# Cross attention block, one core: the first two chunks of scores of a group start behind the turns and the first feed-forward product

## The chip, the cores and the metric

The kernel runs on one core of one Trainium2 chip. Times are device microseconds of the whole execution; the median of three runs of the kernel before is 1809.25 us (1807.23 to 1810.44). The engines are TensorE (PE, with its weight loads as PEld), VectorE (DVE), ScalarE (ACT), GpSimd (POOL) and SyncE (SP), whose queue issues the DMAs.

## The reference, cut to what matters

```python
# x, memory: (128, 128, 256); mask (128, 128, 128); 16 heads of 16; FF = 1024
def _self_attn(x, mask, ...):
    q = (x @ Wq.T + bq).reshape(b, s, H, HD)      # k, v likewise
    score = jnp.einsum('bshd,bthd->bhst', q, k) / math.sqrt(HD)
    score = score + (1.0 - mask[:, None, :, :]) * -1000000000.0
    p = jax.nn.softmax(score, axis=-1)
    o = jnp.einsum('bhst,bthd->bshd', p, v).reshape(b, s, d)
    return o @ Wo.T + bo
tgt1 = _layer_norm(tgt, g1, be1)
tgt = tgt + _self_attn(tgt1, mask, ...)
tgt = tgt + (memory @ Wg.T + bg)
tgt1 = _layer_norm(tgt, g2, be2)
ff = jax.nn.relu(tgt1 @ W1.T + b1) @ W2.T + b2
return tgt + ff
```

## The kernel before, in words

The 128 sequences are taken in 64 groups of two (256 rows). The work of a group is spread over several iterations of one loop, as a software pipeline: iteration i makes the first layer norm of group i + 2, turns and projects q, k and v of group i + 1 ("front"), makes the scores and exponentials of group i ("attn_"), the values, output projection and second layer norm of group i - 1 ("out_"), and the feed-forward part of group i - 2 ("ffn"). An iteration has 13 ticks (TICKS), and each engine has its own list by tick, written out by hand; the tables at the top of the file say at which tick a step stands. An engine works its list strictly in that order, and semaphores join the lists. No scheduler moves anything.

Products keep float32 accuracy with three matmuls each: operands are split into a high and a low part (xT_hi and xT_lo, and so on), and `product` makes low x high, high x low and high x high (L807 to L809). For the scores the same is done by stacking: q and k of a group are copied by nine DMAs of SyncE into q_stack (three) and k_stack (six), so that one matmul multiplies all three pairs. These copies are issued when VectorE has made the low parts q_lo and k_lo (L648, L656).

The scores of a group are 8 chunks of four heads. `scores_of(i, n)` (L859) makes chunk n with two matmuls into bank n % 2 of score_ps. Chunk 0 waits for the copies (q_stacked, k_stacked). Each chunk waits until VectorE has read the chunk two before it, which used the same bank (scores_masked). VectorE masks a chunk and takes the row minimum with four instructions (L608, after a small memset, L605); behind chunk 0's masking its list has xT_lo, the low part of the next group's turned input (L571), which the q product needs. ScalarE makes the exponentials of a chunk (L374), and between them the high parts (L367, L436, L445), the relu of the feed-forward tiles (L419) and the copies of turned tiles (L386, L394). TensorE turns a chunk of exponentials (`turn_chunk`, L873), the inverse sums (`turn_inverses`, L883), and xhat for the next group (`turn`, L824).

`up(i, t)` makes two of the eight tiles of the first feed-forward product, 12 matmuls into ffn_ps; at tick 0 it waits for z_split and for y_summed, with which VectorE has read ffn_ps of the group before (L593). At tick 1 stand chunk 2's scores, then the values of the group before (L899) and the q product.

Of the kernel before, what the change touches and what calls it, by code (L numbers as in the profile page):

```python
# [53 lines left out]
def later(g):  # L54

    return not (isinstance(g, int) and g == 0)

def is_at(i, n):

    return isinstance(i, int) and i == n
# [7 lines left out]
def xattn_block(nc, x, memory, mask, wqT, wkT, wvT, woT, wgT, w1T, w2T,  # L69
# [24 lines left out]
    with ExitStack() as ctx:  # L94
# [685 lines left out]
        def _(pe):  # L780
# [22 lines left out]
            def product(dst, pairs, start=True, stop=True, **more):  # L803

                n = len(pairs)
                for j, (lhs, rhs) in enumerate(pairs):
                    pe.matmul(dst, lhs[1], rhs[0], start=start and j == 0, stop=False, **more)  # L807
                    pe.matmul(dst, lhs[0], rhs[1], start=False, stop=False, **more)  # L808
                    last = pe.matmul(dst, lhs[0], rhs[0], start=False, stop=stop and j == n - 1, **more)  # L809
                return last  # L810

            def cut(pair, *at):
                return pair[0][at], pair[1][at]
# [3 lines left out]
            def seq(b):  # L817
                return slice(b * S, (b + 1) * S)
# [8 lines left out]
            def up(i, t):  # L827

                g, n = i - 2, UP_TICKS.index(t)
                if is_at(i, 2) and n == 0:  # L830
                    pe.wait_ge(split_lo, SPLIT_AT["1"])
                    pe.wait_ge(split_more, MORE_AT["2"])
                if n == 0:
                    pe.wait_ge(z_split, g + 1)
                    if later(g):
                        pe.wait_ge(y_summed, g)
                else:
                    pe.wait_ge(hid_relu, HJ * g + n)
                for j in range(2):
                    f = 2 * n + j  # L840
                    last = product(ffn_ps[:, j * ROWS:(j + 1) * ROWS],
                                   [(cut(w1, ALL, k, slice(f * P, (f + 1) * P)), cut(zT, ALL, k))
                                    for k in range(KT)])
                last.then_inc(hid_ready, 1)

            def scores_of(i, n):

                b, c = divmod(n, CPB)
                if b == 0:
                    if c == 0:  # L850
                        if i < 2:
                            pe.wait_ge(zeros_set, 2 * i + 2)
                        pe.wait_ge(q_stacked, 16 * TERMS * (i + 1))
                        pe.wait_ge(k_stacked, 16 * 2 * TERMS * (i + 1))
                if n >= 2 or later(i):
                    pe.wait_ge(scores_masked, CHUNKS * i + n - 1)

                for k in range(KT):
                    last = pe.matmul(score_ps[n % 2][:, k * 2 * S:(k + 1) * 2 * S],  # L859
                                     q_stack[i % 2][:, c, k, seq(b)],  # L860
                                     k_stack[i % 2][:, c, :, GB * k + b, :],
                                     start=True, stop=True)
                last.then_inc(scores_ready, 1)
# [41 lines left out]
            def iteration(i, norm, front, attn_, out_, ffn):  # L905
                fronts, outs = stages_before(i)
                for t in range(TICKS):
                    if attn_ and t == 0:
                        scores_of(i, 0)
                        scores_of(i, 1)  # L910
                    if attn_ and t in SCORE_TICKS:
                        scores_of(i, SCORE_TICKS[t])
                    if attn_ and t in TURN_TICKS:
# [8 lines left out]
                        turn(by_tile[1], xhat).then_inc(x_turned, 1)  # L922
                    if ffn and t in UP_TICKS:
                        up(i, t)
                    if attn_ and t == 1:
                        scores_of(i, 2)
                    if out_ and t == 1:
# [61 lines left out]
            for name in "qk":  # L989
                shift_product(name)  # L990
            pe.wait_ge(ident_loaded, 16)
            run(pe, iteration)

# [34 lines left out]
```

## Time and profile before

| what | value |
|---|---|
| median of three runs | 1809.25 us |
| the profiled execution | 1808.42 us |
| its span | 1806.8 us |
| TensorE busy | 1752.8 us, 97% |
| ScalarE busy | 1455.3 us, 81% |
| VectorE busy | 1356.8 us, 75% |
| GpSimd busy | 876.4 us, 49% |
| mean DMA rate | 102 GB/s |

A time of the trace is counted from the span's start. A row that stands for several instructions (x4) gives the start of the first and the time until the last one's end. A matmul's record is longer than the distance to the next matmul, since they are pipelined. In brackets stands how long the engine was idle before the row, and what ended that; short idle times carry no bracket.

### The profile page before, as it was taken

To read this page: it belongs to the slowest core of one execution; us is meant where nothing else is said; L and a number is where in the kernel's file an instruction comes from.
4 is the path that set the end of the run, shared out by engine and by line. 5 is a ranking of instruction groups with operands and counts; after the bars stand their busy time and mean duration, and the time that the engine had idled before them with its cause. 6 is when DMAs were issued, how large, how long until landed. Compare 5 with 4: busy or idle time off the path is not lost.

```text
span 1806.8 us, 53745 instructions
## 1 busy us (share of the span) xinstructions
PE 1752.8 (97%) x17972; PEld 1717.7 (95%) x17972; DVE 1356.8 (75%) x6807; ACT 1455.3 (81%) x5577; POOL 876.4 (49%) x910
## 2 busy tenths in 40 slices
PE   5699999999999999999999999999999999999997
PEld 5699999999999999999999999999999999999997
DVE  6677777777777777777777777777777777777772
ACT  4788888787787887888787887887888888887882
POOL 4254454454454455455454454444544444454454
PEclk7899999999999999999999999999999999999999
DMA  7665765755765755755755755755755756756740
GB/s 165 94 94 99 119 93 99 118 92 98 121 91 95 124 89 98 123 89 99 124 88 99 123 88 100 123 87 101 124 85 101 121 87 103 117 90 104 112 72 19
DMA packets 148931, 183.66 MB, mean 102 GB/s; under 512 B 14768, under 2 KB 99120, under 8 KB 148656
## 3 DMA queue, kind: packets, MB, share of 16 engines
q1 hardware_dynamic: 148656, 180.23, 60.6%
q8 instruction: 144, 2.36, 0.6%
q14 instruction: 131, 1.07, 0.2%
HBM read 62.73 MB, written 16.78 MB: 44 GB/s over the span
## 4 chain that ended last, share of the span: by engine, by line
PE 94%; ACT 1%; issue 1%; DMA 0%; DVE 0%; SPq 0%; ACTq 0%
PE ffn_ps L807 13%; PE ffn_ps L808 13%; PE ffn_ps L809 13%; PE turn_ps L873 12%; PE work_ps L807 9%; PE work_ps L809 8%; PE work_ps L808 8%; PE score_ps L859 7%; PE value_ps L899 6%; PE work_ps L824 3%; PE turn_ps L883 2%; ACT scores L374 1%; DMA k_stack<-k_hi 0%; ACT hid L419 0%; SPq L325 0%
## 5 line engine op out<-in xcount | busy, mean ns | idle before, releaser
L374 ACT ACTIVATE scores<-scores,row_min 128x128 f32<-128x128 f32 x2048 | 795.4, 402 | 0.8 <-DVE row_min L608 0.8
L733 POOL TENSOR_TENSOR hT_lo<-hid,hT_hi 128x512 fp32r<-128x512 f32 x256 | 355.5, 1389 | 552.5 <-DVE hT_hi L635 552.5
L386 ACT ACTIVATE probs<-turn_ps 128x512 f32<-128x512 f32 x512 | 305.2, 597 | 254.7 <-PE turn_ps L873 254.7
L608 DVE CUSTOM_DVE_ANT_0 scores<-score_ps,mask_bias 128x128 f32<-128x128 f32 x2048 | 471.5, 286 | 1.9 <-issue 1.9
L374 ACT ACTIVATION_READ_ACCUMULATOR scores<-scores,row_min 128x1 f32 x2048 | 412.7, 202 | 0.0
L873 PE MATMUL turn_ps<-ident,scores 128*128 128x128 f32 x2048 | 308.3, 273 | 5.9 <-ACT probs L386 5.9
L807 PE MATMUL ffn_ps<-zT_hi,w_lo 128*128 128x256 f32 x1024 | 302.3, 295 | 5.0 <-ACT hid L419 4.1
L807 PE MATMUL ffn_ps<-w_hi,hT_lo 128*128 128x256 f32 x1024 | 300.7, 294 | 2.4 <-ACT hid L419 2.4
L808 PE MATMUL ffn_ps<-zT_lo,w_hi 128*128 128x256 f32 x1024 | 285.5, 279 | 0.0
L809 PE MATMUL ffn_ps<-zT_hi,w_hi 128*128 128x256 f32 x1024 | 284.9, 278 | 0.0
L809 PE MATMUL ffn_ps<-w_hi,hT_hi 128*128 128x256 f32 x1024 | 284.6, 278 | 0.0
L808 PE MATMUL ffn_ps<-w_lo,hT_hi 128*128 128x256 f32 x1024 | 284.4, 278 | 0.0
L873 PEld LDWEIGHTS turn_ps<-ident,scores 128*128 128x128 f32 x2048 | 234.8, 140 | 7.2 <-ACT scores L374 6.6
L635 DVE CAST hT_hi<-hid 128x512 fp32r<-128x512 f32 x256 | 110.1, 430 | 160.3 <-ACT hid L419 160.2
L419 ACT ACTIVATE hid<-ffn_ps,vec 128x256 f32<-128x256 f32 x512 | 212.6, 468 | 18.0 <-PE ffn_ps L809 17.9
L859 PE MATMUL score_ps<-k_stack,q_stack 128*128 128x256 f32 x1024 | 199.8, 288 | 24.7 <-issue 13.9
L807 PEld LDWEIGHTS ffn_ps<-zT_hi,w_lo 128*128 128x128 f32 x1024 | 193.9, 189 | 6.6 <-ACT hid L419 5.1
L807 PEld LDWEIGHTS ffn_ps<-w_hi,hT_lo 128*128 128x128 f32 x1024 | 192.7, 188 | 3.0 <-ACT hid L419 3.0
L808 PEld LDWEIGHTS ffn_ps<-w_lo,hT_hi 128*128 128x128 f32 x1024 | 193.8, 189 | 0.0
L808 PEld LDWEIGHTS ffn_ps<-zT_lo,w_hi 128*128 128x128 f32 x1024 | 193.8, 189 | 0.0
L809 PEld LDWEIGHTS ffn_ps<-zT_hi,w_hi 128*128 128x128 f32 x1024 | 192.8, 188 | 0.0
L809 PEld LDWEIGHTS ffn_ps<-w_hi,hT_hi 128*128 128x128 f32 x1024 | 192.2, 188 | 0.0
(113 smaller groups left out, 4242.2 us busy)
## 6 DMA issues: line engine op xcount, KB each, us to landing
q_stack<-q_hi SPq DMA_DIRECT2D x128, 256.0 KB, 6.8
k_stack<-k_hi SPq DMA_DIRECT2D x256, 128.0 KB, 7.3
x_in<-x_dram SPq DMA_DIRECT2D x64, 256.0 KB, 3.7
mem_in<-memory_dram SPq DMA_DIRECT2D x64, 256.0 KB, 7.9
x_res<-x_dram SPq DMA_DIRECT2D x64, 256.0 KB, 7.9
q_stack<-q_lo SPq DMA_DIRECT2D x64, 256.0 KB, 4.2
k_stack<-k_lo SPq DMA_DIRECT2D x128, 128.0 KB, 7.3
out_dram<-y SPq DMA_DIRECT2D x64, 256.0 KB, 2.2
```

Of the source, the lines that this page charges most:

```text
L374: last = act.activation(exps, exps, ACT.Exp, bias=row_min[:, k, h:h + 1], scale=-1.0, accum_out=row_sum[:, k, h:h + 1])
L386: act.activation(probs[:, k, :], turn_ps[k % 2][:, :], ACT.Copy).then_inc(probs_copied, 1)
L419: last = act.activation(hid[:, n % 2, j, :], ffn_ps[:, j * ROWS:(j + 1) * ROWS], ACT.Relu, bias=b1c[:, 2 * n + j:2 * n + j + 1])
L608: last = dve.tensor_tensor_reduce(out=scores[:, slot(i, t), h, :], in0=score_ps[t % 2][:, h * S:(h + 1) * S], in1=mask_bias[:, b, :], scal ...
L635: dve.tensor_copy(hT[0][:, 2 * n:2 * n + 2, :], hid[:, n % 2]).then_inc(hid_hi, 1)
L733: pool.tensor_tensor(halves[1], src, halves[0], ALU.subtract).then_inc(done, 1)
L807: pe.matmul(dst, lhs[1], rhs[0], start=start and j == 0, stop=False, **more)
L808: pe.matmul(dst, lhs[0], rhs[1], start=False, stop=False, **more)
L809: last = pe.matmul(dst, lhs[0], rhs[0], start=False, stop=stop and j == n - 1, **more)
L859: last = pe.matmul(score_ps[n % 2][:, k * 2 * S:(k + 1) * 2 * S], q_stack[i % 2][:, c, k, seq(b)], k_stack[i % 2][:, c, :, GB * k + b, :], ...
L873: last = pe.transpose(turn_ps[k % 2][:, h * S:(h + 1) * S], scores[:, slot(g, k), h, :], ident[:])
L899: last = pe.matmul(value_tiles[32 * c:32 * (c + 1), k, seq(b)], v_pad[g % 2][:, b, head_of(c, h), :], probs[:, CPB * b + c, h * S:(h + 1) ...
```

## The change

On TensorE alone, the scores of chunks 0 and 1 are no longer first in tick 0. They stand at the end of tick 0: behind the turn of the last group's chunk 7, the turn of its inverse sums, the turn of xhat and the first two feed-forward tiles. Chunk 2 stays at tick 1, and so stands right behind them. The lists of the other engines, and what each step waits for, are the same.

```diff
             def iteration(i, norm, front, attn_, out_, ffn):
                 fronts, outs = stages_before(i)
                 for t in range(TICKS):
-                    if attn_ and t == 0:
-                        scores_of(i, 0)
-                        scores_of(i, 1)
                     if attn_ and t in SCORE_TICKS:
                         scores_of(i, SCORE_TICKS[t])
                     if attn_ and t in TURN_TICKS:
...
                         turn(by_tile[1], xhat).then_inc(x_turned, 1)
                     if ffn and t in UP_TICKS:
                         up(i, t)
+                    if attn_ and t == 0:
+                        scores_of(i, 0)
+                        scores_of(i, 1)
                     if attn_ and t == 1:
                         scores_of(i, 2)
                     if out_ and t == 1:
```

The first place is TensorE's list where an iteration begins, behind the last matmul of the group's second feed-forward product. Before:

```order
L809 MATMUL ffn_ps<-w2_hi,hT_hi 128x256
L859 MATMUL score_ps0<-k_stack1,q_stack1 128x256 [waits scores_masked,k_stacked,q_stacked]
L859 MATMUL score_ps0<-k_stack1,q_stack1 128x256
L859 MATMUL score_ps1<-k_stack1,q_stack1 128x256 [waits scores_masked]
L859 MATMUL score_ps1<-k_stack1,q_stack1 128x256
L873 MATMUL turn_ps1<-ident,scores 128x128 [waits probs_copied,exps_ready]
L873 MATMUL turn_ps1<-ident,scores 128x128 x3
```

And of the kernel after the change:

```order
L809 MATMUL ffn_ps<-w2_hi,hT_hi 128x256
L873 MATMUL turn_ps1<-ident,scores 128x128 [waits probs_copied,exps_ready]
L873 MATMUL turn_ps1<-ident,scores 128x128 x3
L883 MATMUL turn_ps0<-ident,inv_rows 128x128 [waits probs_copied,inv_spread]
L883 MATMUL turn_ps0<-ident,inv_rows 128x128 x3
L824 MATMUL work_ps1<-ident,xhat 128x128 [waits z_split,ln1_ready]
L824 MATMUL work_ps1<-ident,xhat 128x128 x3
L807 MATMUL ffn_ps<-zT_hi,w1_lo 128x256 [waits y_summed,z_split]
```

The four score matmuls, with their wait for the copies, are gone from here; the turns follow the second product at once.

The second place is the end of the 12 matmuls of the first feed-forward product and what follows. Before:

```order
L809 MATMUL ffn_ps<-zT_hi,w1_hi 128x256
L859 MATMUL score_ps0<-k_stack1,q_stack1 128x256 [waits scores_masked]
L859 MATMUL score_ps0<-k_stack1,q_stack1 128x256
L899 MATMUL value_ps<-probs,v_pad0 32x128 [waits attn_ready,values_set,probs_copied]
L899 MATMUL value_ps<-probs,v_pad0 32x128 x31
L807 MATMUL work_ps1<-xT_hi,wq_lo 128x256 [waits x_split]
```

And after the change:

```order
L809 MATMUL ffn_ps<-zT_hi,w1_hi 128x256
L859 MATMUL score_ps0<-k_stack1,q_stack1 128x256 [waits scores_masked,k_stacked,q_stacked]
L859 MATMUL score_ps0<-k_stack1,q_stack1 128x256
L859 MATMUL score_ps1<-k_stack1,q_stack1 128x256 [waits scores_masked]
L859 MATMUL score_ps1<-k_stack1,q_stack1 128x256
L859 MATMUL score_ps0<-k_stack1,q_stack1 128x256 [waits scores_masked]
L859 MATMUL score_ps0<-k_stack1,q_stack1 128x256
L899 MATMUL value_ps<-probs,v_pad0 32x128 [waits attn_ready,values_set,probs_copied]
```

Chunks 0, 1 and 2 now stand in a row. The last of them goes to score_ps0, the bank of the first.

## Rows read from the trace of the kernel before

**Rows 1.** The page: its head, and the chain that ended last by engine.

```profile
span 1806.8 us, 53745 instructions
...
PE 94%; ACT 1%; issue 1%; DMA 0%; DVE 0%; SPq 0%; ACTq 0%
```

**Rows 2.** The table of waits: total us, times, longest us.

```profile
PEld score_ps L859 <- issue: 31.9, 49, 5.2
```

**Rows 3.** Timeline of PEld, a group's first scores: start, us, operation, [idle before].

```profile
112.23 0.53 PEld L859 LDWEIGHTS score_ps<-k_stack,q_stack 128*128 128x128 f32 x4 [0.40 <-issue]
...
818.64 0.53 PEld L859 LDWEIGHTS score_ps<-k_stack,q_stack 128*128 128x128 f32 x4 [0.17 <-issue]
...
845.44 0.55 PEld L859 LDWEIGHTS score_ps<-k_stack,q_stack 128*128 128x128 f32 x4
...
1742.35 0.53 PEld L859 LDWEIGHTS score_ps<-k_stack,q_stack 128*128 128x128 f32 x4 [0.42 <-issue]
```

**Rows 4.** Timeline of PE at the start of the group at 845.55 us.

```profile
845.55 0.64 PE L859 MATMUL score_ps<-k_stack,q_stack 128*128 128x256 f32 x4
...
846.03 0.60 PE L873 MATMUL turn_ps<-ident,scores 128*128 128x128 f32 x4
...
847.26 0.36 PE L807 MATMUL ffn_ps<-zT_hi,w_lo 128*128 128x256 f32 x1
...
848.63 0.28 PE L809 MATMUL ffn_ps<-zT_hi,w_hi 128*128 128x256 f32 x1
...
848.75 0.40 PE L859 MATMUL score_ps<-k_stack,q_stack 128*128 128x256 f32 x2
```

**Rows 5.** Timeline of a group whose scores and masks both waited, 655.3 to 657.6 us.

```profile
655.62 0.53 PEld L859 LDWEIGHTS score_ps<-k_stack,q_stack 128*128 128x128 f32 x4 [0.60 <-issue]
655.65 0.71 PE L859 MATMUL score_ps<-k_stack,q_stack 128*128 128x256 f32 x4 [0.42 <-issue]
...
656.21 0.60 PE L873 MATMUL turn_ps<-ident,scores 128*128 128x128 f32 x4
...
656.30 0.06 DVE L605 MEMSET carrier<- 128x1 f32 x1 [0.33 <-PE score_ps L859]
...
657.18 0.08 DVE L608 DVE_READ_ACCUMULATOR2_ANT row_min<- 128x1 f32 x1
```

**Rows 6.** Timeline, 45.5 to 47.5 us: scores that waited for VectorE.

```profile
46.01 0.08 DVE L608 DVE_READ_ACCUMULATOR2_ANT row_min<- 128x1 f32 x1
...
46.15 0.30 PEld L859 LDWEIGHTS score_ps<-k_stack,q_stack 128*128 128x128 f32 x2 [0.70 <-DVE row_min L608]
```

**Rows 7.** Timeline of VectorE and ScalarE, 845.3 to 849.6 us.

```profile
845.75 0.69 DVE L593 TENSOR_TENSOR y<-ffn_ps,resid_b 128x512 f32<-128x512 f32 x1
...
848.03 0.39 ACT L374 ACTIVATE scores<-scores,row_min 128x128 f32<-128x128 f32 x1
...
848.17 0.69 DVE L571 TENSOR_TENSOR xT_lo<-work_ps,xT_hi 128x512 fp32r<-128x512 f32 x1 [0.87 <-ACT xT_hi L367]
```

**Rows 8.** Timelines of ACT and PEld between 825 and 830 us.

```profile
825.83 0.84 ACT L436 ACTIVATE q_hi<-work_ps,qk_bias 128x256 fp32r<-128x256 f32 x2 [0.24 <-PE work_ps L809]
...
828.10 0.83 ACT L419 ACTIVATE hid<-ffn_ps,vec 128x256 f32<-128x256 f32 x2
...
829.61 0.19 PEld L807 LDWEIGHTS ffn_ps<-zT_hi,w_lo 128*128 128x128 f32 x1
```

**Rows 9.** Timelines of VectorE and PE in the first groups.

```profile
55.94 2.34 DVE L543 TENSOR_SCALAR xhat<-x_in,mv,rstd 128x256 f32<-128x256 f32 x2
...
82.38 1.20 PE L859 MATMUL score_ps<-k_stack,q_stack 128*128 128x256 f32 x4 [4.38 <-issue]
...
88.18 0.39 PE L859 MATMUL score_ps<-k_stack,q_stack 128*128 128x256 f32 x2
```

**Rows 10.** The tail: PE's timeline; stretch, busy PE PEld DVE ACT POOL, clock, DMA.

```profile
1789.96 0.38 PE L807 MATMUL ffn_ps<-zT_hi,w_lo 128*128 128x256 f32 x1 [0.93 <-ACT hid L419]
...
1784.00:1800.00 16.00, 11.41 (x91) 10.44 (x90) 3.10 (x6) 3.96 (x9) 6.83 (x6) 1.00 0.05 18
```

## The prediction

> **What bounds the kernel now.** I read the page first. TensorE carries 94% of the chain that ended last, and no other engine more than 1% [rows 1]. So a microsecond in which TensorE waits is a microsecond of time, and one that another engine gains or loses counts only where TensorE waits for it. The second view is the table of waits: beside the start-up, TensorE's repeated wait is ahead of the scores (49 times, 31.9 us, put down to "issue") [rows 2]. The third view is the row of the four score matmuls that open a group. They stand once a group, and their weight loads start at 112.23 us for group 3 and at 1742.35 us for group 63: 60 periods of (1742.35 - 112.23) / 60 = 27.17 us [rows 3]. Of these 60 starts, 44 carry a mark of an idle stretch of 0.17 to 0.60 us. The start at 845.44 us carries none, and its period is 845.44 - 818.64 = 26.80 us [rows 3]. The code says what it is: the first chunk waits for the six copies into k_stack, and these land just about when TensorE gets there.
>
> **What the change removes.** The two chunks that wait for those copies are started later: behind three sets of four turns and behind the two tiles of the first feed-forward product. In the group without a wait the scores take 846.03 - 845.55 = 0.48 us, the turns 847.26 - 846.03 = 1.23 us and the product 848.75 - 847.26 = 1.49 us [rows 4]. The copies thus get 1.23 + 1.49 = 2.72 us more, where they were at most 0.6 us late. I show below that their issue slides by at most about 1.5 us relative to a group's start, while a whole period grows too; so this wait goes. Its worth: the free period is 26.80 us from load to load, but a load that has waited stands 0.08 us nearer to its matmul, so from matmul to matmul it is up to 26.88 us. The gain is 0.29 to 0.37 us a group, middle 0.33; times 61 groups (3 to 63) that is 20 us, bounds 18 to 22.
>
> **What the change adds.** score_ps has two banks. Chunk 2 writes the bank of chunk 0 and waits for scores_masked, that is for VectorE to have read chunk 0. Before, 2.72 us of other matmuls stood between chunk 1 and chunk 2, and the wait was met long before. Now chunk 2 stands right behind chunk 1 (second pair of order fences), and nothing covers it. I lay this out on the times of [rows 4]. The turns start where the scores did, at 845.55. The product starts 0.48 earlier than it did, at 846.78, and its last matmul at 848.63 - 0.48 = 848.15. Chunk 0's two matmuls start at 848.27 and 848.39, and the second ends 0.28 later, at 848.67. Chunk 1 is through TensorE's order at 848.75, the very time at which chunk 2 started before, since it is the same work in another order.
>
> How long VectorE then needs is shown by a group in which VectorE stood waiting for the scores [rows 5]. The four matmuls there start at 655.65 and the last at 655.65 + 0.71 - 0.28 = 656.08, so chunk 0's second started near 655.84 and ended near 656.12; VectorE's first instruction starts at 656.30, a hop of 0.18 us. Its last accumulator read ends at 657.18 + 0.08 = 657.26, which makes 0.96 us for a chunk. From VectorE's end to the weight load that waited for it the trace has one clean place: 46.01 + 0.08 = 46.09 to 46.15, 0.06 us [rows 6]. Chunk 2's load is released at 848.67 + 0.18 + 0.96 + 0.06 = 849.87, that is 1.12 us behind 848.75. A load that is released by a wait isn't done ahead of time: in [rows 5] it takes 656.21 - 655.62 = 0.59 us from the load to the next group of matmuls, where 0.48 is usual. That is 0.11 us more. The stall is 1.12 + 0.11 = 1.23 us; with a hop of 0.14 in place of 0.18 it is 1.19, and without the restart it is 1.08. I take 1.2 us, bounds 1.05 to 1.3. Times 61 groups: 73 us, bounds 64 to 79.
>
> **What is queued behind it.** VectorE must be free when chunk 0 lands: its sum for the output y runs from 845.75 to 846.44 [rows 7], and nothing else of its list stands before chunk 0's masking, so it is. The same sum frees ffn_ps for the product, which would now start at 846.78; that leaves about 0.3 us, the closest cover on this side. If it fell short, the turns and the product would slide by what lacks, so it is no gain for anyone. Behind the masking stands xT_lo, 0.69 us long, which before ran at 848.17 [rows 7] and now ends near 849.8 + 0.7 = 850.5. The q product needs it, but the 64 matmuls of the values stand ahead of that product and take about 1.9 us from 850.2, so this is hidden.
>
> ScalarE starts chunk 0's exponentials at 848.03 before [rows 7] and near 849.80 now, 1.77 us later; it had idle time ahead of them, and of q_hi another 0.24 us [rows 8]. By q_hi it is some 1.5 us late against 1.2 us of TensorE. The next thing that TensorE wants of it is the second tiles' relu: it runs 828.10 to 828.93, and TensorE's load that needs it starts at 829.61 [rows 8]. Of the 0.68 us between them 0.3 to 0.35 us goes, so it still holds. Through q_lo and k_lo, which follow ScalarE, the copies are issued those 1.5 us later, against 1.2 + 2.72 = 3.9 us later that they are wanted. ScalarE's lateness ends in its idle time near the end of a group, where it waits for turns that TensorE makes late in its order. I cost these at nothing, with 0 to 0.2 us a group (12 us) kept for the upper end.
>
> **The first groups.** Group 0: VectorE is busy with weights, and its first masks start no earlier; nothing. Group 1: xhat for its turns is ready only at 55.94 + 2.34 = 58.28 [rows 9], behind the landing of the copies, so what is saved in one place is lost in the other; nothing. Group 2 waited 4.38 us for its copies; turns and product now run in that time. Its chunk 2 started at 88.18, and would start about 1.8 us behind 82.38 [rows 9], some 4 us earlier. But the exponentials come only about 2.5 us earlier, and some of the values then fall into the stretch at half clock. I take 2.5 us of gain, bounds 0 to 4.
>
> **Sum.** +73 - 20 - 2.5 = +50.5 us. The profiled execution took 1808.42 us with a span of 1806.8 us: 1808.4 + 50.5 = 1859 us. The median of the runs before, 1809.25, lies 0.8 above that execution, which changes nothing here.
>
> **A rule that speaks of such waits.** After the waits of 0.93 us in the last two iterations, the granted clock stayed at 1.00, the 2.4 GHz level, over 1784 to 1800 us though they came every 2.6 us or so [rows 10]; after the 4.38 us wait the same work went at the 1.2 GHz level: from 82.38 to 88.18 = 5.80 us, for what takes 848.75 - 845.55 = 3.20 us otherwise [rows 4, 9]. The Trainium skill, "TensorE: Matmul & The Clock Gate", section "A second HAM failure mode: psum-queue depth-cycling", tells of a kernel in which short idle times between groups of matmuls while the PSUM banks are cycled let the clock swing. By that rule each of the new waits could set the clock back; by the rows of the tail it would not. No trace here has a wait of 1.2 us once a group in the steady part.
>
> **Rivals.**
> 1. The clock falls at each new wait. If each costs what the half clock cost behind 82.38, 5.80 - 3.20 = 2.6 us: 61 x 2.6 = 159 us more, 2018 us. Against it stands the tail [rows 10]. 2%.
> 2. ScalarE becomes a second thing to wait for. Its lateness against TensorE eats more than the 0.68 us of [rows 8], and the feed-forward tiles wait 0.3 to 0.5 us a group: 61 x 0.4 = 24 us more, 1883 us. For it: ScalarE runs without a break from q_hi to the end of the group. Against it: the 0.3 us left. 7%.
> 3. The wait for the copies stays, since q_lo and k_lo slide with ScalarE: then the 20 us aren't gained, 1879 us. It would take a slide of over 3 us. 3%.
> 4. The other side: faster. Chunk 2 isn't held up, because its mark is set before TensorE gets there; then only the gains are left, 1808.4 - 20 - 2.5 = 1786 us. It decides at the second matmul of chunk 0: VectorE's reading would have to end within 0.36 us of its start, where [rows 5, 6] give 0.28 + 0.18 + 0.96 + 0.06 = 1.48. Something between (a stall that later waits give back) would need idle time of TensorE to be paid from, and in the steady part there is hardly any other than the one that I have already counted. 4%, with 1% of it all for a draw.
>
> **How the numbers follow.** My forecast has 83%, the rivals 7, 3, 2 and 4% and a draw 1%. 0.2% (3.6 us) is about what a measurement of this kernel can tell from no change. Slower by more than that: 83 + 7 + 3 + 2 = 95%; within it 1%; faster 4%. The range: all terms low, 64 - 22 - 4 = +38, 1846 us; all high, 79 - 18 + 12 = +73, 1881 us. All at one end at once is unlikely; I let it begin a little lower, at 1844, for a smaller restart and hop, and end at 1878.
>
> **What would show it.** Right: no idle mark ahead of the group's first scores; chunk 2's weight load waiting for row_min at 1.0 to 1.3 us once in every group; VectorE's masks of chunk 0 right behind the first two scores, with idle time before them; periods near 26.84 + 1.2 = 28.0 us; the granted clock at 1.00; the product's and the down product's waits for ScalarE still rare. Wrong: a period under 27.3 us (the stall isn't there or is repaid), one over 28.4 us (rivals 1 or 2), or a wait that still names k_stack.

## The result, and the profile after

| | before | after |
|---|---|---|
| median | 1809.32 us | 1860.62 us (1858.68 to 1862.06, 4 runs) |
| ratio | | 1.0284, 95% interval 1.0266 to 1.0302 |
| profiled execution, its span | 1808.42, 1806.8 us | 1859.95, 1858.3 us |
| period of a group, groups 3 to 63 | 27.17 us | 28.04 us |

The change made the kernel 51.3 us slower, where 50.5 were forecast. Of the experiments below, one execution of e1 (7810.56 us) and one of e4 (1983.98 us, at a granted clock of 0.88, the profiled one, so no row of e4 is shown) were far slower than the others, and the ratios leave them out. In the page after, the chain of work that ended last answers to [rows 1]; VectorE has come into it:

```profile
span 1858.3 us, 53745 instructions
...
PE 92%; DVE 4%; ACT 2%; issue 1%; DVEq 0%; ACTq 0%
```

The table of waits after (total us, times, longest us) answers to [rows 2]. The 49 waits of the first scores are gone, and in their place TensorE's load waits for VectorE at chunk 2 once in every group, with one more in group 0; VectorE waits for the scores and ScalarE for VectorE about as often:

```profile
DVE carrier L605 <- PE score_ps L859: 150.6, 66, 2.8
...
ACT scores L374 <- DVE row_min L608: 137.1, 64, 2.8
PEld score_ps L859 <- DVE row_min L608: 76.1, 65, 2.1
PE score_ps L859 <- DVE row_min L608: 63.1, 65, 1.8
```

The timeline of one group after, from chunk 0's scores to the values, answers to [rows 4, 5]. The row of x4 is chunks 0 and 1 and has no mark of idle time; the next row of PE is chunk 2:

```profile
868.84 0.53 PEld L859 LDWEIGHTS score_ps<-k_stack,q_stack 128*128 128x128 f32 x4
868.95 0.62 PE L859 MATMUL score_ps<-k_stack,q_stack 128*128 128x256 f32 x4
869.50 0.06 DVE L605 MEMSET carrier<- 128x1 f32 x1 [2.35 <-PE score_ps L859]
...
870.39 0.08 DVE L608 DVE_READ_ACCUMULATOR2_ANT row_min<- 128x1 f32 x1
...
870.51 0.40 ACT L374 ACTIVATE scores<-scores,row_min 128x128 f32<-128x128 f32 x1 [2.15 <-DVE row_min L608]
870.53 0.30 PEld L859 LDWEIGHTS score_ps<-k_stack,q_stack 128*128 128x128 f32 x2 [1.17 <-DVE row_min L608]
870.53 0.50 PE L859 MATMUL score_ps<-k_stack,q_stack 128*128 128x256 f32 x2 [0.97 <-DVE row_min L608]
...
870.96 0.43 PE L899 MATMUL value_ps<-probs,v_pad 128*32 128x128 f32 x8
```

VectorE's chain is 870.39 + 0.08 - 869.50 = 0.97 us, and 0.06 us later TensorE's load is released. The mark in the timeline is only 0.97 us, but the stall costs more than its mark. Chunk 1 is through TensorE's order at 868.95 + 0.48 = 869.43, while the record of its last matmul runs to 868.95 + 0.62 = 869.57, so TensorE has nothing to issue for 870.53 - 869.43 = 1.10 us. And the load isn't done ahead: from chunk 2 to the values it takes 870.96 - 870.53 = 0.43 us, where it takes 0.32 us in e2 below, which doesn't wait there.

The granted clock, last but two in the row of the steady stretch, stayed at the 2.4 GHz level with these waits in every group:

```profile
120.00:1780.00 1660.00, 1602.82 (x16572) 1571.68 (x16571) 1232.84 (x6280) 1330.21 (x5154) 793.08 (x829) 1.00 0.61 100
```

### The profile page after: what moved, and what is told of

Its sections match the earlier page's. It is cut to its first block, busy times and chain, and to the rows that moved or that the text cites. A ratio compares the mean times of both kernels' runs of the same rounds, so it can differ in the third digit from the quotient of the medians.

```text
span 1858.3 us, 53745 instructions
## 1 busy us (share of the span) xinstructions
PE 1759.2 (95%) x17972; PEld 1718.1 (92%) x17972; DVE 1348.6 (73%) x6807; ACT 1447.0 (78%) x5577; POOL 876.7 (47%) x910
## 4 chain that ended last, share of the span: by engine, by line
PE 92%; DVE 4%; ACT 2%; issue 1%; DVEq 0%; ACTq 0%
PE ffn_ps L807 13%; PE ffn_ps L809 13%; PE ffn_ps L808 13%; PE turn_ps L873 12%; PE work_ps L807 9%; PE work_ps L809 8%; PE work_ps L808 8%; PE score_ps L859 7%; PE value_ps L899 6%; PE work_ps L824 3%; DVE scores L608 2%; PE turn_ps L883 1%; ACT scores L374 1%; DVE xhat L543 0%; DVE row_min L608 0%
## 5 line engine op out<-in xcount | busy, mean ns | idle before, releaser
L859 PE MATMUL score_ps<-k_stack,q_stack 128*128 128x256 f32 x1024 | 201.6, 289 | 63.1 <-DVE row_min L608 63.1
L859 PEld LDWEIGHTS score_ps<-k_stack,q_stack 128*128 128x128 f32 x1024 | 151.6, 190 | 76.7 <-DVE row_min L608 76.1
```

## The experiments

Each run was timed beside the kernel before, whose median was 1807.61 us beside e1 to e4, and 1808.85 us beside e5 to e7. Periods are from the timeline of PE, means over groups 3 to 63. For e2, e5 and e7, where nearly all are equal, the one that repeats is given (26.79, 28.73 and 26.87 us); the means are 26.78, 28.74 and 26.86.

### e1: chunk 2 behind the values

```diff
 # the changed kernel, TensorE's list
-                    if attn_ and t == 1:
-                        scores_of(i, 2)
                     if out_ and t == 1:
                         values_of(i - 1)
+                    if attn_ and t == 1:
+                        scores_of(i, 2)
```

> The changed kernel with chunk 2's scores put behind the 64 matmuls of the values (about 1.9 us), nothing else moved. Theory (the loss is chunk 2 waiting for VectorE to have read chunk 0, since nothing stands between them on TensorE): the wait of 1.0 to 1.1 us a group is covered, the wait for the copies stays away, and the period falls to about 26.85 us: 1787 us, 22 below the kernel before. Rival (the late start of chunks 0 and 1 itself costs, because ScalarE and VectorE get their work 1.8 us later): the time stays above 1840 us, with waits for ScalarE in place of the one for row_min. A second rival: chunk 2 becomes late for VectorE and ScalarE, and a part of the stall comes back at chunk 3 or at a turn: 1800 to 1820 us.

Measured: 1832.48 us, ratio 1.0134 (1.0119 to 1.0150), period 27.60 us. Neither the theory's 1787 nor the rivals' 1840 and more or 1800 to 1820. The wait for row_min is gone, as the theory said, and another stands in its place. In the trace of e1, at the third pair of feed-forward tiles (answers to [rows 8]):

```profile
863.54 0.83 ACT L419 ACTIVATE hid<-ffn_ps,vec 128x256 f32<-128x256 f32 x2
...
864.42 0.19 PEld L807 LDWEIGHTS ffn_ps<-zT_hi,w_lo 128*128 128x128 f32 x1 [0.74 <-ACT hid L419]
864.42 0.39 PE L807 MATMUL ffn_ps<-zT_hi,w_lo 128*128 128x256 f32 x1 [0.50 <-ACT hid L419]
```

So the late start of chunk 0 has a price of its own. ScalarE begins the exponentials at 857.00, 4.26 us behind the first turn at 852.74, where before it was 848.03 - 845.55 = 2.48 us behind the group's start: 1.78 us late, as forecast. From there to the end of that relu, 863.54 + 0.83 = 864.37, its rows carry no idle mark, so it isn't kept waiting for the later chunk 2: it works without a break and began too late. In the changed kernel TensorE itself slips by 1.25 us at chunk 2, and ScalarE's lateness hides behind that slip. With the slip gone, it shows.

### e2: chunks 0 and 1 behind the turns only

```diff
 # the changed kernel, TensorE's list
                         turn(by_tile[1], xhat).then_inc(x_turned, 1)
+                    if attn_ and t == 0:
+                        scores_of(i, 0)
+                        scores_of(i, 1)
                     if ffn and t in UP_TICKS:
                         up(i, t)
-                    if attn_ and t == 0:
-                        scores_of(i, 0)
-                        scores_of(i, 1)
```

> Half of the move: chunks 0 and 1 stand behind the three sets of turns, but ahead of the two tiles of the first feed-forward product, which again lie between chunk 1 and chunk 2. Theory: the turns give the copies 1.23 us, more than the 0.6 us they were late at most, and the product's 1.49 us cover VectorE's chain of 1.2 us behind chunk 0, so neither wait is left: period 26.85 us, 1788 us. Rival (the wait for the copies slides along with whatever stands ahead of it, because their issue follows ScalarE): it stays at 0.3 us a group, 1809 us, no change.

Measured: 1786.05 us, ratio 0.9878 (0.9862 to 0.9893), period 26.79 us. The theory holds, and this version beats both kernels. From group 3 on its scores wait for nothing. In its timeline chunk 2's load (866.62) stands 0.19 us behind the end of chunk 0's masking (866.35 + 0.08), so the product covers the chain, but only just; and ScalarE's exponentials begin at 866.47, 2.9 us behind the first turn (864.81 - 1.23 = 863.58), so ScalarE is late by 0.4 us instead of 1.8:

```profile
864.81 0.72 PE L859 MATMUL score_ps<-k_stack,q_stack 128*128 128x256 f32 x4
...
865.46 0.06 DVE L605 MEMSET carrier<- 128x1 f32 x1 [0.99 <-PE score_ps L859]
...
866.35 0.08 DVE L608 DVE_READ_ACCUMULATOR2_ANT row_min<- 128x1 f32 x1
...
866.62 0.30 PEld L859 LDWEIGHTS score_ps<-k_stack,q_stack 128*128 128x128 f32 x2
```

### e3: the kernel before, with the wait for the copies shortened

```diff
 # the kernel before; counts of k_stacked from 16 * 2 * TERMS to 16 * 2 * 2
-                        for j, high_low in enumerate((0, 1, 0)):
+                        for j, high_low in enumerate((0, 1)):
```

> The kernel before, in its order, with the third copy of k into k_stack left out (four copies a group in place of six; the product of low q with high k is missing from the scores). It prices the wait for the copies alone: they land about 1.3 us earlier. Theory: the wait ahead of a group's first scores is gone, 0.33 us a group, and each of the first three groups starts about 1 us earlier: 1809 - 20 - 3 = 1786 us. Rival (the marks of idle time ahead of the scores are another cause, such as TensorE's own restart): the marks and the time stay, 1806 us or more.

Measured: 1784.67 us, ratio 0.9870 (0.9857 to 0.9884), period 26.85 us. The theory holds: the mark ahead of the first scores was the copies' landing, and its whole price is 27.17 - 26.85 = 0.32 us a group and 112.27 - 105.08 = 7.2 us up to the scores of group 3, where 3 us were expected. Of such waits the table of waits of TensorE has only a few left, in the first groups:

```profile
PE score_ps L859 <- DMA k_stack<-k_lo: 6.2, 2, 4.2
```

### e4: the kernel before, with chunks 0, 1 and 2 in a row

```diff
 # the kernel before, TensorE's list
                     if attn_ and t == 0:
                         scores_of(i, 0)
                         scores_of(i, 1)
+                        scores_of(i, 2)
...
-                    if attn_ and t == 1:
-                        scores_of(i, 2)
```

> The kernel before, with chunk 2's scores right behind chunks 0 and 1 at the start of the iteration; the turns and the product follow. It has the stall of the changed kernel without its gain. Theory: chunk 2 waits for VectorE as in the changed kernel, 1.2 us and up to 0.2 us more where VectorE is still at the sum for y, and the wait for the copies is as before: 64 groups x 1.3 = 83 us, 1892 us. Rival (in the changed kernel it is the place of chunks 0 and 1 that costs, not the row of three): no or little change, 1809 to 1830 us.

Measured: 1892.41 us, ratio 1.0466 (1.0452 to 1.0480). That is 84.8 us over the kernel before, 1.3 us a group. Chunks 0 and 1 stand where they always stood, so it is the row of three that costs, in both places where it was tried.

### e5: two more masking instructions ahead of chunk 0's four

```diff
 # the changed kernel, VectorE's list
+                        if t == 0:
+                            for n in range(2):
+                                dve.tensor_tensor_reduce(
+                                    out=xhat2[:, 0, n * S:(n + 1) * S],
+                                    in0=score_ps[0][:, n * S:(n + 1) * S],
...
                         for h in range(CH):
```

> The changed kernel with two more of the masking instructions ahead of chunk 0's four, into a tile that is free there: the dose test of VectorE's chain. Theory (TensorE waits for exactly this chain): 2 x 0.21 = 0.42 us a group more, x 64 = 27 us: 1887 us, and the wait marked row_min grows from about 1.0 to 1.4 us. Rival (VectorE's chain is hidden and something else sets the end, the hand-over or ScalarE): 1861 to 1865 us.

Measured: 1908.40 us, ratio 1.0549 (1.0534 to 1.0563), period 28.73 us, 0.69 us more than after the change. The mark at chunk 2 grew by the dose, from 0.97 to 1.39 us:

```profile
889.50 0.06 DVE L606 MEMSET carrier<- 128x1 f32 x1 [2.35 <-PE score_ps L867]
...
890.96 0.50 PE L867 MATMUL score_ps<-k_stack,q_stack 128*128 128x256 f32 x2 [1.39 <-DVE row_min L616]
```

In the table of waits the sum went from 63.1 to 89.9 us, the 27 us of the theory. But the time grew by 47.8 us (by 44.4 between the spans of the two profiled executions), so the measured time lies 21 us above the theory's 1887. The other 0.27 us a group carry no mark. They lie in small parts over the rest of the group; from the turn at 878.80 to that at 883.96, for instance, it takes 5.16 us, where after the change it takes 863.96 - 858.97 = 4.99. It is the spacing of the matmuls: those of 128x256 that follow each other without a wait (less than 150 ns apart, groups 5 to 59) stand 117.2 ns apart on the mean in e5, and 115.2 to 115.5 ns in the kernel before, the changed kernel, e1 to e3, e6 and e7. Some 147 of them a group make 147 x 1.9 ns, about 0.28 us. e6 and e7 ran on the same chip as e5, and the granted clock is 1.00 in all of them, so neither tells them apart. That TensorE waits for VectorE's chain one for one is shown; why the matmuls stood wider apart is not.

### e6 and e7: ScalarE's relus earlier, in the kernel of e1

```diff
 # e6: the kernel of e1, ScalarE's list (relu() is the old body)
-                    if ffn and t in RELU_TICKS:
+                    if ffn and t in RELU_TICKS and t != 3:
                         relu(i, RELU_TICKS.index(t))
...
                         last.then_inc(q_high, 1)
+                    if ffn and t == 2:
+                        relu(i, 1)
 # e7: e6, and relu() at tick 7 ahead of copy_turned() at tick 7
```

> The kernel of e1 (chunk 2 behind the values, 1832 us) with ScalarE's second relu put ahead of the exponentials of chunk 2. Theory (ScalarE is late as a whole, by some 0.75 us more than TensorE can bear, because chunk 0's exponentials start 1.8 us later): the wait ahead of the third pair of feed-forward tiles goes, but the next thing that TensorE wants of ScalarE, the fourth relu ahead of the down product, had only 0.28 us to spare in e1 and is then late by about 0.5 us, with the restart 0.6 us: 1787 + 61 x 0.6 = 1824 us, with the mark of ScalarE's relu moved to the down product. Rival (only the place of that one relu is at fault): 1787 us, no such mark left.

Measured: 1815.88 us, ratio 1.0035 (1.0022 to 1.0047), period 27.33 us. The theory's mechanism holds and its size is somewhat too large (1824 expected): the wait didn't go, it moved to the down product, with 0.54 us a group in place of 0.81:

```profile
863.04 0.86 ACT L403 ACTIVATE hid<-ffn_ps,vec 128x256 f32<-128x256 f32 x2
863.95 0.19 PEld L812 LDWEIGHTS ffn_ps<-w_hi,hT_lo 128*128 128x128 f32 x1 [0.51 <-ACT hid L403]
```

> The kernel of e6 with the fourth relu also put ahead of the copy of the turned chunk 3, which is 0.48 us of ScalarE. Theory: 0.48 of the 0.6 us of wait go, 0.1 to 0.2 us a group are left: 1787 + 61 x 0.15 = 1796 us. Rival (only the place of the second relu was at fault in e1): the same as e6, at 1787 us.

Measured: 1786.36 us, ratio 0.9875 (0.9861 to 0.9888), period 26.87 us. The second relu that was brought forward took the rest away, more fully than the 0.1 to 0.2 us that I had left. With both waits covered, the changed kernel's place for chunks 0 and 1 is as good as e2's. The two differ by 0.3 us, which is nothing, though not by the same parts: e2's period is 0.08 us shorter, and e7 is ahead at the start, with the first turns of group 3 at 106.32 us against 113.56.

## Why the prediction was right, step by step

**The wait for the copies goes: right.** No group from 3 to 63 has a mark ahead of its first scores. Its worth was taken as 0.33 us a group; e2, with neither wait, runs at 26.79 us, so it is 27.17 - 26.79 = 0.38, just over the bound of 0.37. By e3, which takes away this wait alone and leaves the order as it was, it is 0.32. The forecast lies between them.

**Chunk 2 waits for VectorE: right, in place and size.** Against the free period of e2 the stall is 28.04 - 26.79 = 1.25 us; against e7, which has chunks 0 and 1 in the very place of the changed kernel, it is 28.04 - 26.87 = 1.17 us. The layout gave 1.23, of which I took 1.2 for the sum; the hop from TensorE to VectorE was 0.15 here (869.35 to 869.50, by the same reckoning as from [rows 5]), the chain 0.97, the hop back 0.06. e4 has a stall of about this size (1.3 us) without the move, e5 gives it a dose, e1 and e2 take it away by putting work between.

**What stands behind it costs nothing: right for this kernel.** ScalarE's exponentials came 1.78 us late. The second relu ran at 849.00 to 849.83 and TensorE's load for it was at 850.36:

```profile
849.00 0.83 ACT L419 ACTIVATE hid<-ffn_ps,vec 128x256 f32<-128x256 f32 x2
```

So 0.53 of 0.68 us were left, where I had expected 0.33 to 0.38. But the prediction should have said what that margin rests on. It holds only as long as TensorE loses its own 1.2 us at chunk 2. I used this to cost ScalarE's lateness at nothing, and forgot it when I wrote what e1 would do; that expectation was 45 us too low for exactly this reason. The move has two prices, 1.25 us by VectorE and 27.60 - 26.79 = 0.81 us by ScalarE (1.17 and 0.73 us against e7), and they stand side by side: together they cost 1.25.

**The rivals.** The clock didn't fall at the waits of about 1 us: the granted clock is 1.00 over the whole steady part. The Trainium skill, "TensorE: Matmul & The Clock Gate", section "A second HAM failure mode: psum-queue depth-cycling", has short idle times between groups of matmuls make the clock swing; the trace doesn't bear this out for waits of 1 us once in 28 us. ScalarE as a second wait (rival 2) didn't come in this kernel, but is real, as e1 shows. The copies didn't slide with ScalarE far enough to matter (rival 3), and nothing made chunk 2's mark come early (rival 4).

**The start-up.** Here the forecast was 2.5 us of gain. The first turns of group 3 started near 111.82 - 2.72 = 109.10 us, where its scores started at 112.27: 3.2 us. A part of this comes by a way that I hadn't seen. Before, the clock stood at half in the stretch behind the long wait; after the change the turns and the product stand in that wait, and the clock was at 1.00. First the kernel before, then after:

```profile
82.00:86.00 4.00, 3.62 (x17) 3.65 (x18) 0.97 (x9) 0.60 (x1) 0.00 (x0) 0.50 0.57 189
```

```profile
82.00:86.00 4.00, 3.03 (x29) 2.54 (x31) 1.68 (x12) 1.28 (x4) 0.00 (x0) 1.00 0.65 206
```

That the work in the wait is what kept the clock up isn't shown. In e2, which has only the turns there, it was at 0.50 in this stretch; but in e7, which has the turns and the product there, it was at 0.50 from 76 to 80 us.

**The sum.** 60 periods give 60 x (28.04 - 27.17) = 52 us; the start-up takes back 3.2; the stretch from the last group's start (2.72 us ahead of its scores) to the end is longer by 67.0 - 64.4 = 2.6 us. That makes 51.4, against 51.5 us between the two spans. The prediction had 1.2 us for it, the stall of the last of its 61 groups. But by the same reckoning this stretch takes 66.5 us in e7, which has no stall, and 65.8 in e2. So most of the 2.6 us comes with the later scores and not with the last stall; how it comes about wasn't tried. That the forecast of the whole is off by only 0.8 us is in part luck: the gain of the start-up was taken 0.7 us too small, and the end 1.4 us too short.

## What to carry to other kernels

When a step is moved to cover a wait, look at what it was itself covering: here two banks allow two chunks in flight, and the third needs as much other work ahead of it as the reader of the first takes (0.15 + 0.97 + 0.06 us). Move the waiting step just far enough past work that is ready, and leave the rest between it and its successor: the turns alone (1.23 us) were enough for copies that were at most 0.6 us late. And a margin that was worked out with one wait in place isn't there once that wait is removed, so the slack of the next engine is to be reckoned anew for each version.

## What the runs showed that I had not expected

- Two extra VectorE instructions of 0.21 us cost 0.69 us a group, 0.42 of it in the wait that they lengthen. The remainder is in matmuls that stand 117.2 ns apart in place of 115.3, and its cause stays open.
- Without the two waits the period repeats: 59 of 60 are 26.79 us in e2 and 26.87 us in e7, all 60 are 26.85 us in e3. In the kernel before it went from 26.88 to 27.46 us from group to group. e3 shows that the wait for the copies makes this scatter; that the copies' landing and the group's start chase each other is my reading.
- ScalarE's lateness can't be bought off at one place: in e6 the wait moved from the third pair of tiles to the down product, and only the second reordering, 0.48 us of it, brought 29.5 us.
